# Expert stage of an audio tower layer: TensorE's slot loop written out, the gather issued ahead of the store, row normalisation moved to the end of VectorE's slot

## What is computed

```
x = layernorm(h).reshape(-1, 256)                 # 16*255 = 4080 token rows
gates = softmax((x @ w_red) @ wg_n.T); idx = argmax; scores = max
h1 = gelu(x @ W1[idx] + b1[idx])                  # 256 -> 512, 8 experts
o  = (h1 @ W2[idx] + b2[idx]) * scores            # 512 -> 256
out = h + o
```

## Time and profile before

| What | Value |
|---|---|
| median of 3 runs | 593.19 us (591.73 to 594.14) |
| the profiled execution | 592.6 us, its span in the trace 590.8 us |
| TensorE matmul busy | 527.1 us, 89% of the span |
| VectorE busy | 471.5 us, 80% |
| ScalarE, GpSimd busy | 229.7 us (39%), 197.6 us (33%) |
| mean granted clock of TensorE | 0.98 of full |
| DMA | 43.04 MB, mean 73 GB/s |

### The profile page before, as it was taken

How to read it: one execution, slowest core, us unless ns; L and a number is a source line. 1 busy time by engine, 2 the same in 40 slices (tenths; PEclk the granted TensorE clock), 3 DMA queues, 4 the chain that set the end, 5 groups by cost and what they waited for, 6 DMA issues and landing times. The chain is left out here.

```text
span 590.8 us, 12977 instructions
## 1 busy us (share of the span) xinstructions
PE 527.1 (89%) x3457; PEld 371.3 (63%) x3458; DVE 471.5 (80%) x1212; ACT 229.7 (39%) x439; POOL 197.6 (33%) x276
## 2 busy tenths in 40 slices
PE   2988999999999999999869799999588988988982
PEld 2865667777666677776526666675355765765661
DVE  2757888898888888988998999997667877877771
ACT  1335445455654544656443211111033433434440
POOL 2463232322223222221230222231225555555532
PEclk9989999999999999999989999999879999999997
DMA  9211212221222122111231233323412222222210
GB/s 252 97 37 37 73 40 67 71 71 36 71 71 68 39 71 71 57 50 36 50 113 44 89 98 108 117 73 126 161 36 71 74 62 76 62 63 68 65 43 1
DMA packets 32682, 43.04 MB, mean 73 GB/s; under 512 B 7234, under 2 KB 23859, under 8 KB 32400
## 3 DMA queue, kind: packets, MB, share of 16 engines
q1 hardware_dynamic: 22604, 28.11, 15.0%
q0 software_dynamic: 3744, 9.34, 5.5%
q10 hardware_dynamic: 6308, 5.28, 3.1%
HBM read 34.02 MB, written 9.59 MB: 74 GB/s over the span
## 5 line engine op out<-in xcount | busy, mean ns | idle before, releaser
L518 PE MATMUL banks<-proj,xnT_h 128*128 128x512 f16 x384 | 115.6, 383 | 6.2 <-DVE early L1220 6.2
L499 PE MATMUL banks<-early 128*128 128x256 f16 x768 | 88.5, 276 | 2.6 <-DVE wo_l L1049 2.6
L499 PEld LDWEIGHTS banks<-early 128*128 128x128 f16 x768 | 76.0, 99 | 12.0 <-DVE wo_l L1049 2.9
L518 PE MATMUL banks<-proj,xnT_l 128*128 128x512 f16 x192 | 73.3, 382 | 0.0
L518 PEld LDWEIGHTS banks<-proj,xnT_h 128*128 128x128 f16 x384 | 37.5, 98 | 43.5 <-DVE early L1220 7.4
L1848 POOL DMA_INDIRECT out<-proj,vo x39 | 39.6, 1016 | 65.2 <-DVE vo L1679 47.9
L747 PE MATMUL banks<-w2h,vo 128*128 x312 | 57.6, 273 | 4.0 <-DVE proj L1677 3.5
L728 PE MATMUL banks<-w1h,vo 128*128 x156 | 54.5, 391 | 7.4 <-issue 4.9
L1842 POOL DMA_INDIRECT vo<-token_rows,vo x39 | 42.4, 1086 | 28.0 <-issue 28.0
L996 ACT ACTIVATE vo<-banks 128x256 f16<-128x256 f32 x39 | 15.0, 384 | 90.9 <-PE banks L715 66.5
L1833 POOL TENSOR_TENSOR rows<-rows,minus_half 128x1 f32 x32 | 23.5, 735 | 74.9 <-DVE rows L1517 74.9
(11 more groups left out here) (258 smaller groups left out, 1276.3 us busy)
## 6 DMA issues: line engine op xcount, KB each, us to landing
early<-in_x SPq DMA_DIRECT2D x16, 512.0 KB, 3.4
stage<-in_W SPq DMA_DIRECT2D x32, 256.0 KB, 2.8
early<-lam_by_chunk SPq DMA_DIRECT2D x32, 132.0 KB
token_rows<-rows ACTq DMA_DIRECT2D x16, 129.0 KB, 2.6
rows<-in_b SPq DMA_DIRECT2D x1, 2048.0 KB, 7.0
token_rows<-rows ACTq DMA_DIRECT2D x16, 112.9 KB, 2.0
vo<-in_tok_W ACTq DMA_DIRECT2D x2, 512.0 KB, 7.1
early<-lam_by_head SPq DMA_DIRECT2D x16, 64.0 KB
```

What stands on the lines that cost most here:

```text
L499: last = mm(bank(2 + j, D), x_[:, k, at:at + P], w[:, KG * half + k, :], start=(half == 0 and k == 0 and x_ is gT_h and w is wtok_h), stop ...
L518: last = mm(dst, a, c, start=(i == 0), stop=(i == n - 1))
```

## The change

TensorE's helper `slots` with its loop goes; all 39 slots are written out, each expert number is read once, in the slot ahead, and stays in its register. On VectorE `norm_rows(i+2)` moves from the place between `split_rows(i+1)` and `scaled_bias(i)` to the end of the slot, behind `split_gelu(i-1)` and `finish(i-2)`. On GpSimd the wait for `y_done` stands alone in `done`, and the gather is issued ahead of the store. VectorE's, ScalarE's and GpSimd's loops stay.

```diff
-            def slots(g, count=RING, first=False, last=False):
-                i0 = RING * g
-                experts = {0: expert_of(i0)}
-                for w in range(count):
-                    up(i0 + w, experts[w])
-                    if w + 1 < count:
-                        experts[w + 1] = expert_of(i0 + w + 1)
-                    if w < 2 and not first:
-                        experts[w - 2] = expert_of(i0 + w - 2)
-                    ...
-            with pe.Fori(1, ROUNDS) as g:
-                slots(g)
+            experts = {0: expert_of(0)}
+            for i in range(SLOTS):
+                up(i, experts[i])
+                if i + 1 < SLOTS:
+                    experts[i + 1] = expert_of(i + 1)
+                    transpose_rows(i + 1)
+                if i >= 1:
+                    transpose_gelu(i - 1, (i - 1) % 2)
+                if i >= 2:
+                    down(i - 2, i % 2, experts[i - 2])
@@ VectorE, slots
                         split_rows(i + 1)
-                    if not (last and w >= count - 2):
-                        norm_rows(i + 2, (w + 2) % RING, g if w + 2 < RING else g + 1)
                     scaled_bias(i, w, e)
                     if not (first and w == 0):
                         split_gelu(i - 1, (w - 1) % 2)
                     if not (first and w < 2):
                         finish(i - 2, (w - 2) % RING, g - 1 if w < 2 else g)
+                    if not (last and w >= count - 2):
+                        norm_rows(i + 2, (w + 2) % RING, g if w + 2 < RING else g + 1)
@@ GpSimd
-                    store(RING * g_ + w, w)
+                    done(RING * g_ + w)
                     load(w, ring_ids[:, w, 1:2])
+                    store(w)
```

More of the change, by code:

```diff
@@ L749, in down @@
                 last.then_inc(s["m2_ready"], 1)
-            def slots(g, count=RING, first=False, last=False):
-                i0 = RING * g
-                experts = {0: expert_of(i0)}
-                for w in range(count):
-                    up(i0 + w, experts[w])
-                    if w + 1 < count:
-                        experts[w + 1] = expert_of(i0 + w + 1)
-                    if w < 2 and not first:
-                        experts[w - 2] = expert_of(i0 + w - 2)
[L762 to L768, removed]
             pe.wait_ge(s["experts_ready"], 1)
             transpose_rows(0)
-            slots(0, first=True)
-            with pe.Fori(1, ROUNDS) as g:
-                slots(g)
[L775 to L778, removed]
+            experts = {0: expert_of(0)}
[8 more added lines that the diff above has]
+                    down(i - 2, i % 2, experts[i - 2])
+            transpose_gelu(SLOTS - 1, (SLOTS - 1) % 2)
+            for i in (SLOTS - 2, SLOTS - 1):
+                down(i, i % 2, experts[i])
         @block.scalar
@@ L1844, in load, with done, store @@
                                         bounds_check=B * NTOK - 1, oob_is_err=False).then_inc(s[f"row_in_{w}"], 16)
-            def store(i, w):
+            def done(i):
                 pool.wait_ge(s["y_done"], apart(pool, i + 1))
+            def store(w):
                 pool.indirect_dma_start(out_rows, bass.IndirectOffsetOnAxis(ap=ring_ids[:, w, 0:1].bitcast(U32), axis=0),
@@ L1858, in _ @@
                 for w in range(RING):
-                    store(RING * g_ + w, w)
+                    done(RING * g_ + w)
                     load(w, ring_ids[:, w, 1:2])
+                    store(w)
             for w in range(RING + REST):
-                store(RING * (ROUNDS - 1) + w, w % RING)
+                done(RING * (ROUNDS - 1) + w)
                 if w < REST:
                     load(w, ring_ids[:, w, 1:2])
+                store(w % RING)
             for w in range(RING):
```

## The result

The changed kernel takes **601.42 us** (median of 4 runs, 600.15 to 604.32) against 593.26 us for the kernel before on the same chip: a ratio of 1.0147, 95% interval 1.0105 to 1.019. It is slower, and outside the forecast's range of 586 to 597.5 us. The profiled execution has a span of 599.2 us (600.98 us with what lies around it), where the sum of the prediction amounts to a span of 589.4.

What follows compares the result with a forecast made beforehand. TensorE was taken as near its limit but losing 12 us to round-start gaps and late gathers. After the change, 35 slots at 3.66 us plus 1.1 us put the end 1.4 us sooner: median 591.8 us, range 586 to 597.5.

Steps and rivals of the forecast that it cites:

- the sum of the prediction: Whole kernel: transpose_rows(38) 1.4 us sooner, nothing changed behind it, so profiled execution 591.2 us and median 591.8.
- TensorE written out: TensorE's round starts: gaps of 1.20 + 1.13 us go, at most 14 us; about nine more instruction fetches, hidden.
- Gather ahead of the store: GpSimd: gather 1.32 us sooner, store that much later at no cost; VectorE's 11.3 us of waiting for rows goes.
- The ring of the third edit: Chain of waits from norm_rows through TensorE, ScalarE and finish to the next norm_rows: 3.66 us a slot, binding.
- TensorE's pace: Rival: the new chain of waits does not bind, slots go at TensorE's 3.29 us, 577.7 us; chance 0.09.
- The start: First slots: split_gelu stays at 438.01 and norm_rows(3) follows at 438.61, from where 35 slots are counted.
- to `finish(i-1)` 0.60: Link on VectorE from split_gelu to finish, 0.60 us of the 3.66 us a slot.
- the rival of the register read: VectorE's expert-number read held until norm_rows starts: at most 0.44 us a slot, 607 us; chance 0.10 shared with fetches.
- VectorE's back-edges: VectorE's five loop returns: 0.22 us each, 1.1 us in all, bounds 0 and 0.6 each.
- The rule weighed in the prediction: Skill's rule that taken branches can force fetches, so full unrolling is preferred; the prediction found the trace agreeing only in part.

Runs made afterwards that it cites:

- e5: Changed kernel without the gathers of slots 6 to 38, that work left out: 587.41 us, ratio .9944 to the kernel before.
- e6: Changed kernel without the stores of slots 0 to 32, that work left out: 587.71 us, ratio .9962 to the kernel before.
- e2: Changed kernel with norm_rows back in its old place, TensorE written out and gather first kept: 578.25 us, ratio .9785 to the kernel before.
- e3: Changed kernel with the store ahead of the gather again, TensorE written out and norm_rows last kept: 594.85 us, ratio 1.0053 to the kernel before.
- e1: Kernel before with only TensorE's slots written out: 587.87 us, ratio .9945.
- e12: Changed kernel with norm_rows in its old place and VectorE's five rounds written out too: 584.98 us, ratio .9854 to the kernel before.
- e7: Changed kernel gathering 8 bytes a row in place of 1032, both issues a slot kept: 603.01 us, ratio 1.0223 to the kernel before.
- e8: Changed kernel with GpSimd holding each store until the next down's signal is there: 594.53 us, ratio 1.0083 to the kernel before.
- e11: Changed kernel with norm_rows one place earlier, behind split_gelu but ahead of finish: 583.55 us, ratio .9867 to the kernel before.

## Why the prediction was wrong

**What held.**
- *TensorE written out.* Its back-edge gaps went and new instructions had to be fetched: the profile counts 19 fetches where it counted 13 before, 6 more where about nine were forecast, and no cost of them is seen (e5 has them all and keeps the ring's pace). TensorE is idle at L715 in 36 slots, as forecast.
- *Gather ahead of the store.* No wait for gathered rows is left, and the final store is not late: from `transpose_rows(38)` at 578.03 to the end it is 21.2 us, as before (569.64 to 590.8).
- *The ring of the third edit.* It was worked out as 3.66 us. In half of the slots of the changed kernel, and in nearly all of e5 and e6, `norm_rows` to `norm_rows` is 3.65: in e5 443.68 to 447.32 (3.64). With the back-edges of VectorE, 128.2 to 128.3 us for 35 slots; the forecast had 35 x 3.66 + 1.1 = 129.2.
- *The order of the versions.* That the third edit gives back what the first two bring is shown by e2: 578.25 us, where the rival "TensorE's pace" had 577.7 for a kernel without the ring.

**The start** was 1.2 us too late in the sum, and that was luck. `norm_rows(3)` follows `split_gelu(0)` by 0.61 us, as forecast, but `split_gelu(0)` starts at 436.82 in place of 438.01. The clock rose earlier in this execution: over 427 to 442 us the granted clock was 0.89 of full, before 0.77, and the second `up` took 1.31 us to the transposes in place of 2.53, with its matmuls 0.22 us apart in place of 0.43. e2, e3 and e5, with the same code on TensorE, had 0.77.

**The step that failed** is the one on the gather: "The wait for `y_done` stays, GpSimd issues as much as before, two indirect DMAs a slot, and no other queue is passed", with nothing counted against it but the store's own lateness, and with it the ring's link "to `finish(i-1)` 0.60", which took `down`'s signal as on time. What the runs showed in its place: in the ring GpSimd keeps a fixed phase. The gather starts 1.4 us after `finish` starts (444.27 to 445.70) and the store 2.8 after (447.05), while the signal that the next `finish` needs is due at 447.11 + 0.29 = 447.40, 3.1 after. So the store's issue of 1.03 us lies over it in 33 slots, and the signal comes 0.4 or 1.1 us late. Going through the ring link by link in the changed kernel, against the median lengths in e5: `finish` is late by 9.1 us in sum, `gelu` by 2.7, and each of the rest by 0.4 or less. 9.1 + 2.7 is 11.8 of the 140.14 - 35 x 3.65 = 12.4 us that the 35 slots took too long. Ring 10.9 over the forecast, start 1.2 under it: 9.7, and the span is 599.2 against 589.4.

**The 2.7 us of `gelu`** look like the rival of the register read, and its measure even fits: `add_bias` stands 0.45 us behind `norm_rows` in most slots of e5, 0.54 to 0.81 in most of the changed kernel, and 1.15 to 1.25 in the first slot of four rounds (0.73 to 0.77 in e5). Those four slots alone hold 1.9 of the 2.7 us. So VectorE's back-edges, put at 1.1 us in all, took 0.6 in e5 and 2.3 in the changed kernel, four of them close to the bound of 0.6 each. But the sequencer isn't held by `norm_rows`, as that rival had it: e5 and e6 have the same order and the same read, and only 5 such waits with 1.5 us in place of 31 with 11.5. It is held by the instruction ahead, `finish`, whose signal is missing. In the eight kernels with `norm_rows` last the register read never starts before `down`'s signal: in 271 slots it starts 0.13 to 0.92 us after it, at the same place of a round by nearly the same amount whether the signal is early or late (0.8 in the first slot of a round), and `add_bias` 0.80 to 1.34 us after the read, as at 449.56 for the signal of 448.53. e3 parts the signal from `finish`: ahead of its slots 12, 18, 24 and 30 the signal is 0.38 to 0.42 us late, `finish` starts 0.61 behind `split_gelu` as if it were not, and `add_bias` still stands 1.09 to 1.17 behind `norm_rows`. So a late signal costs twice: where `finish` itself is late, and, even where `split_gelu` hides it from `finish`, at the back-edges.

**The rule weighed in the prediction**, that branches cost fetches and kernels are better unrolled (the Trainium skill, "Runtime: NRT & Kernel Launch", "Instruction fetch mechanics"), agrees with e1 (.9945) and does not with e12, which is e2 written out further (.9854 against .9785). The pace of the slots was better there, and the phase against GpSimd worse.

**What is not settled.** The runs show that the signal is on time when no issue lies at that phase (e5, e6), that the bytes gathered do not matter (e7), that moving the issue takes most of the loss away (e8), that nearly all late signals are due beside the second of two close issues, and that they come out at two fixed times of an issue. They don't show what in the chip holds the signal, nor what chooses between the two times; and a signal due less than 0.77 us into a first or single issue did not occur. The Trainium skill, "Perfetto Trace Analysis", "Tensor Engine Instruction (MATMUL, LD_WEIGHTS)", puts two steps between a matmul's reported end and the moment others see its semaphore: the acknowledgement of the written bytes, and the propagation of the update. A delay in either would look like this one; it gives no figure and names no cause, and no run here tells the two apart.

## What to carry to other kernels

When a step closes a ring within one slot, every signal in it counts with its own delay, and slack that used to hide a late one is gone: work out not only the lengths of the links but what else runs at the moment at which each signal is due. An edit that "issues as much as before" still moves its issues in time; draw GpSimd's indirect DMAs beside the signals of the ring, and if a signal falls 0.25 to 1.45 us into the second of two close ones, move it or take the waiting instruction out of the ring, as e11 does: its ring is 20 us shorter. And try the parts of a change alone: two of the three edits together were 2.2% faster, all three 1.5% slower.

## What the runs showed of the hardware that was not expected

- The semaphore signal of a matmul came 0.29 us after the matmul's start in all 39 slots of e5 and e6, and 0.64 to 0.72 or 1.40 to 1.47 us after it where it was due 0.37 us into the second of two indirect DMA issues that start 1.3 us apart; in e2 and e12, due just ahead of one, up to 2.1 us. Due 0.77 to 1.05 us into a first or single issue, none of 135 was late.
- An indirect DMA holds GpSimd for about 1.02 us, whether it gathers 1032 B a row or 8 B, and the next starts 1.3 us after it at the soonest.
- A register read behind an instruction of VectorE that waits for a semaphore started 0.13 to 0.92 us after that semaphore's signal in 271 slots, and never before it.
- A wait that is put down to an engine which had long finished can be a wait for its late signal: "DVE proj L1664 <- PE banks L747" with the matmul's end 1.17 us before it (447.38 and 448.55).
